# Placing two groups' tokens in PSUM during the alignment passes, in a cross-attention and feed-forward kernel

## The reference

```
D = sqrt(|a|^2 + |b|^2 - 2 a.b)            # a: 64 context rows, b: 512 normalised tokens
R[i,j] = D[i,j] + min(R[i-1,j], R[i,j-1], R[i-1,j-1])
path   = backtrack(R)                       # from (63, 511) to (0, 0)
x1     = x + sum of ctx[i] over the path's cells (i, j), for each token j
h      = relu(quant(quant(layernorm(x1)) @ w1q.T + b1q))
out    = x1 + h @ w2q.T + b2q
```

## Time and profile before

| what | value |
|---|---|
| median of three runs | 191.31 us |
| the profiled execution, whole | 189.99 us |
| its span, first to last instruction | 188.2 us |
| DVE busy | 153.4 us (82%) |
| ACT busy | 104.0 us (55%) |
| PE matmul busy | 98.8 us (52%) |
| mean granted TensorE clock | 0.80 of full |

### The profile page before, as it was taken

The page is one execution under the profiler, slowest core; times in us unless marked ns, Lnnn a source line. Parts: engine busy times, 40 slices in busy tenths (PEclk is TensorE's granted clock), DMA queues, the critical chain, the costliest instruction groups (busy, mean ns, idle before and its releaser), DMA issues.

```text
span 188.2 us, 3726 instructions
## 1 busy us (share of the span) xinstructions
PE 98.8 (52%) x1230; PEld 68.0 (36%) x1239; DVE 153.4 (82%) x746; ACT 104.0 (55%) x192; POOL 37.6 (20%) x97
## 2 busy tenths in 40 slices
PE   0689871000062000000000968887999999998991
PEld 0678770000041000000000334644666666665671
DVE  1994955999999999999999099797988989996351
ACT  3787675699994000053150019668686867777720
POOL 8964473000000000000000000011232505132250
PEclk9999998555555555555555799999999999999999
DMA  4994002900049800010112321004427456373857
GB/s 163 350 348 147 3 9 59 401 16 0 2 157 337 291 0 0 0 69 2 70 61 80 56 35 24 0 0 56 59 22 90 53 66 59 56 86 34 102 57 169
DMA packets 19603, 16.89 MB, mean 90 GB/s; under 512 B 5760, under 2 KB 19200, under 8 KB 19456
## 3 DMA queue, kind: packets, MB, share of 16 engines
q1 hardware_dynamic: 14336, 12.69, 21.0%
q0 software_dynamic: 3808, 3.67, 16.6%
q10 hardware_dynamic: 1440, 0.30, 0.8%
HBM read 7.48 MB, written 9.18 MB: 88 GB/s over the span
## 4 chain that ended last, share of the span: by engine, by line
DVE 46%; PE 40%; issue 5%; ACT 5%; DMA 3%; DVEq 0%; SPq 0%
PE y L1231 12%; PE h L1214 6%; DVE Y L1014 6%; DVE R L807 5%; PE t L1214 3%; DVE A L775 3%; DVE enter L1001 3%; DVE bcarry L1000 3%; DVE carry L795 3%; DVE M L796 3%; DMA X<-in_x_dram 3%; PE h L1127 3%; PE e L1175 3%; PE t L1127 2%; PE y L1099 2%
## 5 line engine op out<-in xcount | busy, mean ns | idle before, releaser
L467 POOL DMA_DIRECT2D out_dram<-E x14 | 17.0, 1217 | 135.3 <-DVE E L985 135.3
L1231 PE MATMUL y<-w2T,XT 128*128 128x256 bf16 x256 | 37.7, 273 | 0.4 <-DVE XT L975 0.4
L1231 PEld LDWEIGHTS y<-w2T,XT 128*128 128x128 bf16 x256 | 25.0, 98 | 14.7 <-DVE XT L975 0.7
L1244 PE MATMUL y<-w1T 128*128 128x512 bf16 x18 | 5.7, 464 | 45.7 <-DVE S_lo L1028 45.7
L622 ACT ACTIVATE h_int<-h,b_s 128x512 int16<-128x512 f32 x37 | 25.4, 686 | 5.6 <-PE h L1214 5.0
L1214 PE MATMUL h<-M,w1T 128*128 128x512 bf16 x68 | 20.6, 380 | 2.3 <-ACT M L615 2.1
L628 ACT ACTIVATE code<-Y,shifts 128x640 bf16<-128x640 bf16 x3 | 2.5, 829 | 31.1 <-DVE enter L1001 31.1
L1244 PEld LDWEIGHTS y<-w1T 128*128 128x128 bf16 x19 | 2.0, 117 | 48.4 <-DVE S_lo L1028 45.5
L975 DVE TENSOR_SCALAR XT<-h_int 128x1024 bf16<-128x1024 int16 x28 | 12.1, 439 | 9.0 <-ACT h_int L622 9.0
L1164 PE MATMUL t<-ident_bf,w_raw 128*128 128x128 bf16 x32 | 4.6, 312 | 22.8 <-ACT w_raw L567 21.2
L622 ACT ACTIVATE h_int<-t,b_s 128x512 int16<-128x512 f32 x19 | 13.0, 686 | 3.2 <-PE t L1214 2.9
(11 more groups left out here) (195 smaller groups left out, 266.9 us busy)
## 6 DMA issues: line engine op xcount, KB each, us to landing
X<-in_x_dram SPq DMA_DIRECT2D x8, 512.0 KB, 8.3
out_dram<-b_s SPq DMA_DIRECT2D x7, 512.0 KB, 5.6
out_dram<-E POOLq DMA_DIRECT2D x14, 256.0 KB, 4.4
w_raw<-in_L_ffn_w_dram SPq DMA_DIRECT2D x2, 1024.0 KB, 5.9
S<-in_ctx_dram SPq DMA_DIRECT2D x1, 512.0 KB, 4.0
out_dram<-E SPq DMA_DIRECT2D x4, 128.0 KB, 2.9
path_dram<-A SPq DMA_DIRECT2D x3, 160.0 KB, 1.8
path_dram<-XT SPq DMA_DIRECT2D x3, 160.0 KB, 1.9
```

Of the source, the lines that this page charges most:

```text
L467: nc.gpsimd.dma_start(tiles_out[:, b:b + 2, quad_of(g), :], res[:, g % 2, 2 * h:2 * h + 2, :], accum_op=ALU.add).then_inc(out_stored[g % 2 ...
L1231: mm = nc.tensor.matmul(bank67[t // 2][:, t % 2, :], hq[:, g % 2, n, t * P:t * P + P], w2T[:, n, :], start=(n == 0 and not bias), stop=(n ...
```

## The change

Six things are edited.

- Group 0's and group 1's tokens are put into PSUM by PE, as the product of an fp32 identity with `X`, during DVE's passes. `align` then adds the context onto them (its first matmul no longer clears). Group 0 uses four banks (e0, e1, y0, y1), group 1 two (h0, t5).
- DVE's adds for groups 0 and 1 are gone. Group 0's statistics are read from PSUM. ACT copies the sums to `X` instead: `copy_sums(j)` two copies of 128x256 for each half of group 0, `copy_next` two of 128x512 for group 1.
- PE aligns groups 0 and 1 one after the other, group 2 before the second half's hidden layer, and transposes group 1 after that half's step 5 instead of at its end.
- The dummy matmuls are 15, 5 and 2 instead of 10, 7 and 2, and start when the flags of slots 2 to 9 are there (`cells_done` at 2), not after `S_lo`.
- Loads of quads 0 and 1 are split by end: SP loads e = 0, ACT e = 1, each waiting only for the stores of its end (but the last piece).
- DVE's order around group 0 and 1 is new; ACT takes group 1's root after the second half's step 0 instead of step 3.

```diff
-WARM = (10, 7, 2)
+WARM = (15, 5, 2)
+        early_bank = [bank01[0], bank5]
+        def early_sum(g, j, h):
+            return (bank23, bank67)[j][h][:, 0, :] if g == 0 else early_bank[h][:, D * j:D * j + D]
...
-                sp.wait_ge(path_out[p], 32)
+                sp.wait_ge(path_out[p][0], 16)
+            for k in range(2):
+                for h in range(2):
+                    for cc in range(CQ):
+                        load_path(sp, k, h, 0, cc)
+            for e in range(2):
+                sp.wait_ge(path_out[INNER + 1][e], 16)
...
+            def copy_sums(j):
+                act.wait_ge(sums_read, 2 * j + 2)
+                for h in range(2):
+                    nc.scalar.activation(X[:, 2 * j + h, :], early_sum(0, j, h), ACT.Copy).then_inc(sums_copied[0], 1)
+            def copy_next():
+                act.wait_ge(aligned, 4)
+                for h in range(2):
+                    nc.scalar.activation(X[:, 4 + h:8:2, :], early_bank[h][:, :].rearrange("p (j d) -> p j d", j=2),
+                                         ACT.Copy).then_inc(sums_copied[1], 1)
...
-                act.wait_ge(path_out[p], 32)
+                act.wait_ge(path_out[p][1], 16)
             for k in range(2):
-                for e in range(2):
+                for h in range(2):
                     for cc in range(CQ):
-                        load_path(act, k, 1, e, cc)
+                        load_path(act, k, h, 1, cc)
             act.wait_ge(b_clip, 2)
+            copy_sums(0)
             deviation_half(0)
+            copy_next()
             copy_half(0)
+            copy_sums(1)
             deviation_half(1)
...
-                if n == 3:
+                if n == 0:
                     deviation(1)
...
-            def spread_half(j):
+            def spread_half(j):
+                v.wait_ge(aligned, j + 1)
                 for h in range(2):
-                    v.wait_ge(x1_ready, 2 * j + h + 1)
-                    nc.vector.bn_stats(stats2[:, 2 * j + h, :], X[:, 2 * j + h, :]).then_inc(dve_order, 1)
+                    nc.vector.bn_stats(stats2[:, 2 * j + h, :], early_sum(0, j, h)).then_inc(sums_read, 1)
...
-            add_half(0)
             spread_half(0)
-            add_half(1)
             quantise_half(0)
             spread_half(1)
-            add_row(1, 0)
             quantise_half(1)
-            add_row(1, 1)
-            clip_half(0, 0)
-            clip_half(0, 1)
             spread_of(1)
-            clip_half(0, 2)
-            clip_half(0, 3)
+            for m in range(NH // 2):
+                clip_half(0, m)
             quantise(1)
+            add_aligned(2)
             for m in range(NH // 2):
-                if m == 2:
-                    add_aligned(2)
                 clip_half(1, m)
...
+            def place_tokens(g):
+                for t in range(4):
+                    if g == 0:
+                        nc.tensor.matmul(early_sum(g, t // 2, t % 2), ident[:, :], X[:, t, :], start=True, stop=False)
+                    elif t < 2:
+                        nc.tensor.matmul(early_bank[t][:, :], ident[:, :], X[:, 4 + t:8:2, :], start=True, stop=False)
...
-            pe.wait_ge(ctx_rest, 2)
...
+            for g in range(2):
+                place_tokens(g)
+            pe.wait_ge(cells_done, 2)
...
             keep_warm(WARM[0])
-            align(0, 0)
-            align(0, 1)
+            pe.wait_ge(ctx_rest, 2)
+            for g in range(2):
+                for j in range(2):
+                    align(g, j)
             keep_warm(WARM[1])
-            align(1, 0)
-            align(1, 1)
             tokens_T_half(0)
...
+            for j in range(2):
+                align(2, j)
             for n in range(NH):
                 hidden_half(1, n)
                 if n >= 4:
                     output(0, n - 4)
-                if n in (5, 7):
-                    align(2, n // 2 - 2)
-            tokens_T(1)
+                if n == 5:
+                    tokens_T(1)
```

More of the change, by code:

```diff
@@ L218, in align_ffn_kernel @@
         lengths_made = sem("lengths_made")
-        path_out = [sem(f"path_out{p}") for p in range(len(PIECE_AT))]
+        path_out = [[sem(f"path_out{p}{e}") for e in range(2)] for p in range(len(PIECE_AT))]
         path_in = [sem(f"path_in{k}") for k in range(QUADS)]
@@ L248, in align_ffn_kernel @@
         x1_ready = sem("x1_ready")
+        sums_read = sem("sums_read")
+        sums_copied = [sem(f"sums_copied{g}") for g in range(2)]
         var2_ready = sem("var2_ready")
@@ L294, in store_path @@
             flags, at = (A, lo) if e == 0 else (flags_rev, SLOTS - hi)
-            queue.dma_start(path_dram[e].ap()[:, at:at + hi - lo, :], flags[:, at:at + hi - lo, :]).then_inc(path_out[p], 16)
+            queue.dma_start(path_dram[e].ap()[:, at:at + hi - lo, :], flags[:, at:at + hi - lo, :]).then_inc(path_out[p][e], 16)
         def load_path(queue, k, h, e, cc):
@@ L346, in _ @@
             for p in range(INNER + 1):
-                sp.wait_ge(path_out[p], 32)
[L348 to L351, removed]
+                sp.wait_ge(path_out[p][0], 16)
[5 more added lines that the diff above has]
+                sp.wait_ge(path_out[INNER + 1][e], 16)
+            for k in range(2, QUADS):
+                for h in range(2):
                     for e in range(2):
@@ L898, in add_row @@
                 nc.vector.tensor_tensor(xv, bank23[h][:, :, :], xv, ALU.add).then_inc(x1_ready, 1)
-            def add_half(j):
+            def spread_half(j):
+                v.wait_ge(aligned, j + 1)
                 for h in range(2):
-                    v.wait_ge(aligned, 2)
-                    nc.vector.tensor_tensor(X[:, 2 * j + h, :], bank23[h][:, j, :], X[:, 2 * j + h, :], ALU.add).then_inc(x1_ready, 1)
-            def spread_half(j):
-                for h in range(2):
-                    v.wait_ge(x1_ready, 2 * j + h + 1)
-                    nc.vector.bn_stats(stats2[:, 2 * j + h, :], X[:, 2 * j + h, :]).then_inc(dve_order, 1)
-                own[0] += 2
-                v.wait_ge(dve_order, own[0])
+                    nc.vector.bn_stats(stats2[:, 2 * j + h, :], early_sum(0, j, h)).then_inc(sums_read, 1)
+                v.wait_ge(sums_read, 2 * j + 2)
                 for t in range(2 * j, 2 * j + 2):
@@ L919, in quantise_half @@
                 v.wait_ge(std2_ready, j + 1)
+                v.wait_ge(sums_copied[0], 2 * j + 2)
                 link(nc.vector.reciprocal(rstd2[:, 2 * j:2 * j + 2], std2[:, 2 * j:2 * j + 2]))
@@ L941, in spread_of @@
                 for h in range(2):
-                    v.wait_ge(x1_ready, 2 * g + h + 3)
+                    if g == 1:
+                        v.wait_ge(sums_copied[1], h + 1)
+                    else:
+                        v.wait_ge(x1_ready, 2 * (g - 2) + h + 1)
                     for j in range(2):
@@ L1169, in align @@
                 pe.wait_ge(path_in[g // 2], 16 * 8)
-                if g >= 1 and j == 0:
-                    pe.wait_ge(x1_ready, 2 * g + 2)
+                if g == 2 and j == 0:
+                    pe.wait_ge(tokens_quantised, 2)
+                    pe.wait_ge(sums_copied[0], 2)
+                if g >= 3 and j == 0:
+                    pe.wait_ge(x1_ready, 2 * (g - 2))
+                early = g < 2
                 for part, third in enumerate((S_hi, S_mid, S_lo)):
@@ L1174, in align @@
                         at = I * h
-                        mm = nc.tensor.matmul(bank23[h][:, j, :], PB[at:at + I, g, 2 * j + h, :],
-                                              third[at:at + I, batch_of(g, 2 * j) // 2, :], start=(part == 0), stop=(part == 2))
+                        sums = early_sum(g, j, h) if early else bank23[h][:, j, :]
+                        mm = nc.tensor.matmul(sums, PB[at:at + I, g, 2 * j + h, :],
+                                              third[at:at + I, batch_of(g, 2 * j) // 2, :], start=(part == 0 and not early),
+                                              stop=(part == 2 and (g != 1 or j == 1)))
                 mm.then_inc(aligned, 1)
@@ L1200, in hidden_half @@
                     pe.wait_ge(xqT_copied, j + 1)
+                    pe.wait_ge(sums_copied[1], 2)
                 if i >= 3:
@@ L1220, in output @@
                 t, n0 = part // 2, (part % 2) * (NH // 2)
+                if part == 0 and g == 0:
+                    pe.wait_ge(sums_copied[0], 4)
                 if g == 0 and t % 2 == 0:
@@ L1239, in _ @@
             pe.wait_ge(wT_copied, NH)
+            pe.wait_ge(prods_made, 4 * LOADS)
+            pe.wait_ge(std_ready, LOADS)
+            pe.wait_ge(sum_copied, LOADS)
+            for g in range(2):
+                place_tokens(g)
+            pe.wait_ge(cells_done, 2)
             def keep_warm(count):
                 for i in range(count):
-                    nc.tensor.matmul(bank67[0][:, :, :].rearrange("p j d -> p (j d)"), w1T[:, 0, 0:P], w1T[:, 0, 0:512],
```

(9 more changed lines are left out.)

## The result

The changed kernel took 188.18 us (median of four runs, 187.87 to 188.70), the kernel before 191.42 us (four runs, 190.46 to 192.04). The ratio is 0.9857, 95% interval 0.9824 to 0.9891. The gain is 3.2 us in the medians. Between the two profiled executions, 189.99 and 187.87 us, the gain is 2.1 us.

What follows compares the result with a forecast made beforehand. DVE bounds the two passes, then a chain of waits to group 2's hidden layer, gated by flag loads. Loads, dummies and placement 0, group 2 1.2 us earlier: median 191.31 to 190.1, range 189.0 or a little below to 191.6.

Steps and rivals of the forecast that it cites:

- Loads split by end: Flag loads before group 0's alignment: gate stays at 107.0, gain 0; bounds 0.4 us earlier, 0.3 later.
- Earlier dummies: PE's dummy matmuls before the alignment: done by 105.8, at worst 107.6; gain 0, since DMA is the gate.
- rival A: Dummies before alignment: earlier ones also remove the cost of a late clock rise in the runs; median about 189.0; chance 0.18.
- First half of group 0: DVE's statistics directly after alignment, from PSUM: 107.55 instead of 108.55, 1.0 us earlier; PSUM reads cost 0 to 0.15 more.
- ACT's new work: ACT's copies ahead of group 0's root: 0.36 us each, root at 109.07 instead of 109.88, reciprocal 1.0 us earlier.
- rival B: ACT's queue after alignment: copies at full cost take most of the gain; median 190.8; chance 0.17.
- Group 1 and group 2: After group 0: group 1's hidden layer at 122.0 instead of 123.22, group 2's reciprocal 124.5 instead of 125.78; sum 1.2 us.
- Placement under the passes: PE placing tokens in PSUM during DVE's passes, 3.9 us or about 8 at half clock: hidden, cost 0.
- Rival C: PE's pauses around group 0 drop the clock: 2.1 us slower, 193.4; chance 0.13 together with any later gate of loads.

Runs made afterwards that it cites:

- the last experiment: Changed kernel with 8 more dummies, started at 97.1 us when the flags of piece 2 are made: 187.58 us, ratio 0.9868 to the kernel before.
- the repeated run: The changed kernel measured again with nothing altered, against the kernel before: 187.38 us, ratio 0.9833.

## Why the prediction was wrong

The steps that failed are the two terms that were put at 0 ahead of the alignment, the gate of the loads and the earlier dummies. Behind it one term was mis-sized, ACT's copies.

**Loads split by end: failed.** The step said that the gate stays at 107.0 and put at most 0.4 us on it. It came 0.76 us earlier. The split was rightly taken as worthless (0.9839 without it, 1.0004 alone). What moved the gate was that ACT's store landed 0.65 us earlier, because DVE's instruction packet was no longer in its way. The prediction took the store's 2.5 us as the price of such a store. The page of before had a warning that it passed by: the larger stores of the passes, 160 KB each, landed in 1.8 and 1.9 us. (The same page gives 1.9 us for SP's 128 KB beside ACT's. That is no evidence: before, the two stores share a semaphore, and where they do not, in the kernel with split loads, SP's took 2.7 with the packet beside it.)

**Earlier dummies: failed in the median.** Taken as 0, with the clock's late rise as rival A at 0.18. Two readings were behind it. The first dummy was put at 103.69, 0.45 us behind `S_lo`; its weight load is at 103.29, 0.05 us behind, and the rise 3.0 us after it, not 2.6. And one rise was taken for the rule. Over seventeen profiled executions it came 2.8 to 5.9 us after the first dummy; that of before is the third earliest. (The 2.3 us in the expectation of the last experiment is counted from the first matmul recorded.)

Rival A's mechanism is shown. Its 107.96 us is also the alignment's time in the kernel before with 40 memsets, but that is luck: there everything was 0.3 us later, and the prediction's was the end of dummies that it started 0.4 us too late. Against the store the alignment came 6.84 us after it instead of 6.18, 0.7 us late and not 1.0, and the way from there to group 2's transposes took 21.69 us instead of 21.21. On the kernel before the earlier dummies gave 0.4 us in the median, not 1.3, because the loads were late there too (gate 6.27 us). On the changed kernel they give 0.5 to 1.2 us (0.9868 and 0.9895 with late dummies, 0.982 to 0.986 with early ones), and not all that the late rise costs, as the repeated run's gate of 6.27 us shows.

The rest of the distance between profile and median lies ahead of the edit: the store was issued from 99.9 to 102.4 us, in kernels whose work on the critical path is the same up to there.

By the Trainium skill, TensorE: Matmul & The Clock Gate, part 1, the point of the rise does not follow the kernel's start and varies by plus or minus 500 ns. These traces agree that it varies; the size they show is larger, 3.2 us between the earliest and the latest.

**First half of group 0: right.** Statistics 0.55 us after the first alignment (0.54 said). Two statistics from PSUM take 0.76 us, from SBUF 0.74. The estimate from the Trainium skill, VectorE: DVE Perf Modes, section on the TRN2 errata, had 0.13 us for them; the traces show 0.02.

**ACT's new work: right in place, too dear.** Root and reciprocal came where ACT's queue let them. But two copies of 128x256 took 0.66 us and the root started 0.54 us after the first, not 0.72 as from the roundings' 0.36 each. Two such pairs give 0.36 us, nearly all of 1.60 less 1.2. This is the mis-sized term behind the alignment. The sum with ACT's dearer copies (rival B) went the wrong way.

**Group 1 and group 2: right.** PE waited for the clip before group 1's transposes (0.24 us), the first rounding of group 1 and the root behind three roundings set group 2's pace. With the gate's 0.76 and the copies' 0.36 off, every forecast time behind it is met within 0.1 us: transposes 117.67 (118.75 less 1.12 is 117.63), hidden layers 120.93 (120.88) and 128.46 (128.48).

**Placement under the passes: right.** The store was issued at 100.82 and 100.83 in the two traces; PE's 6 us more cost nothing.

**Rival C: did not come.** The clock held at 1.00 through PE's pauses of 0.52 and 0.83 us in the changed kernel, and through one of 1.38 us in the kernel before with early dummies and split loads.

The sum: 1.6 us for the placement and its order by the traces, then 1.0 us (0.9946) for early dummies with the packet out of the way, make 2.6. Measured are 3.0 to 3.3 in the changed kernel and its versions that differ only in the loads or in memsets. The 0.4 to 0.7 us left stay unassigned. Some of it may be the placement: with late dummies, where an earlier landing gives nothing, the changed kernel is still 2.0 and 2.5 us under the kernel before in the medians (0.9895 and 0.9868), not 1.6. The intervals are half a microsecond and more to each side.

Open is why the packet left the store's time. DVE's instructions are the same up to there, and the packets ahead of it come at 65.4 and 83.6 us in both kernels. With 4, 6 and 20 memsets it comes where 101.2 to 101.5 us without any would follow. But with 0 and 2 it comes at 109.6 and 109.2, after DVE's long wait. Between the packet at 83 us and this one the traces have 139 DVE instructions then, against 126 in the kernel before and 128 to 130 with 4, 6 and 20 memsets. That it moved is shown; that the change meant it to, nothing says.

## What to carry to other kernels

A gate made of two waits gives its gain only when both are moved: the earlier landing alone and the split alone gained nothing here, the early dummies little. Before a wait on a small DMA is taken as fixed, look in its window for packets of other queues, instruction packets too, and compare with like transfers. Two stores that share a semaphore have no landing times of their own in the profile. And put dummy matmuls where the latest rise of the clock still fits, by more than one profiled execution; before counting from the first of them, see that its record is there.

## What the runs showed of the hardware

- One instruction packet of DVE's program (8 KB) during two stores of 128 KB held back the last of the sixteen landings of both. That put off their whole landing by 0.6 to 1.0 us, and by 0.2 to 0.4 where the packet came at the stores' start.
- The rise of TensorE's clock from 1.2 to 2.4 GHz came 2.8 to 5.9 us after the first of a row of matmuls of 512 columns, in seventeen profiled executions. The row was unbroken in all but one, which had a pause of about 0.3 us. PE had been idle for 33 to 46 us before it.
- ACT copies two fp32 tiles of 128x256 from PSUM to SBUF in 0.66 us. Two of that shape rounded to int16, with a bias and a scale, take 0.84; which of the differences costs the 0.18 was not tried.
